# Attention projections as five single-pass products of split operands, and expert weights split in eight pieces, in a tokenizer, attention and mixture-of-experts kernel

## What is computed

```python
h = tok_ref(x, freq_bands, W)          # sin and cos of 2 pi x f for 6 bands, (4, 512, 3*6*2*192) @ W.T -> (4, 512, 192)
h = concatenate([cls_tok, h])          # 513 tokens for each of 4 images
h = h + attn(layernorm(h), Wq, Wk, Wv, Wf, bf, Wo, gamma, beta)
h = h + ffn(layernorm(h), ...)         # 8 routed experts, top 2, and a shared expert of 768, mixed by alpha

def attn(x, ...):                      # linear attention with a forget gate, M = 64
    q = (elu(x @ Wq) + 1) / 8;  k = elu(x @ Wk) + 1;  v = x @ Wv
    c = clip(cumsum(log(sigmoid(x @ Wf + bf))), -20, 20)
    M = exp(c) * cumsum(exp(-c) * k v);  z = exp(c) * cumsum(exp(-c) * k)
    h = (q M) / (q z + 1e-6)
    return (norm(h) * gamma + beta) @ Wo
```

## Time and profile before

| | |
|---|---|
| median of 3 runs | 570.83 us (570.6 to 571.26) |
| the profiled execution | 570.71 us |
| its span | 568.9 us |
| PE busy | 555.4 us, 98% |
| DVE busy | 363.0 us, 64% |
| ACT busy | 245.9 us, 43% |
| POOL busy | 174.0 us, 31% |
| L1312, feature projection | 292.0 us in 1,728 records |
| granted PE clock, mean | 0.994 of full speed |

### The profile page before, as it was taken

The page is one execution under the profiler, slowest core; times in us unless marked ns, Lnnn a source line. Parts: engine busy times, 40 slices in busy tenths (PEclk is TensorE's granted clock), DMA queues, the critical chain, the costliest instruction groups (busy, mean ns, idle before and its releaser), DMA issues.

```text
span 568.9 us, 9027 instructions
## 1 busy us (share of the span) xinstructions
PE 555.4 (98%) x3247; PEld 510.8 (90%) x3247; DVE 363.0 (64%) x1040; ACT 245.9 (43%) x343; POOL 174.0 (31%) x200
## 2 busy tenths in 40 slices
PE   5999999999999999999999999999999999999997
PEld 5998999799999989999979899977888889999965
DVE  7736787532968736779761787376787546666537
ACT  3465364654225753442575523254224134545410
POOL 6413133122225311674311461001300504454410
PEclk9998999999999999999999999999998999999999
DMA  8900067000000000210000010330100561531164
GB/s 330 323 21 20 3 216 243 20 10 20 20 18 20 20 0 11 75 56 1 1 0 10 20 37 20 98 126 23 62 2 1 185 206 54 164 95 52 55 199 152
DMA packets 23487, 42.48 MB, mean 75 GB/s; under 512 B 2502, under 2 KB 15044, under 8 KB 23348
## 3 DMA queue, kind: packets, MB, share of 16 engines
q1 hardware_dynamic: 19560, 33.31, 18.1%
q0 software_dynamic: 3472, 8.07, 4.0%
q10 hardware_dynamic: 412, 0.53, 0.4%
HBM read 31.74 MB, written 14.79 MB: 82 GB/s over the span
## 4 chain that ended last, share of the span: by engine, by line
PE 90%; DVE 5%; ACT 3%; DMA 1%; issue 1%; POOL 0%; ACTq 0%; DVEq 0%
PE ps L1312 47%; PE ps L1505 4%; PE ps L1391 2%; PE ps L1557 2%; PE ps L1559 2%; PE ps L1467 2%; PE ps L1469 2%; PE ps L1470 2%; PE ps L1468 2%; PE ps L1471 2%; PE ps L1368 2%; PE ps L1535 1%; PE ps L1537 1%; PE ps L1536 1%; PE ps L1539 1%; PE ps L1538 1%
## 5 line engine op out<-in xcount | busy, mean ns | idle before, releaser
L1312 PE MATMUL ps<-w_tok,feat 128*128 128x192 f32 x1728 | 292.0, 330 | 7.5 <-ACT feat L469 6.3
L1312 PEld LDWEIGHTS ps<-w_tok,feat 128*128 128x128 f32 x1728 | 284.0, 192 | 11.0 <-issue 10.6
L403 POOL TENSOR_SCALAR feat<-fx 128x512 int32<-128x512 f32 x108 | 93.2, 878 | 204.7 <-PE ps L1312 201.3
L478 ACT ACTIVATE feat<-feat 128x1536 f32<-128x1536 f32 x35 | 51.9, 1484 | 118.6 <-DVE feat L773 116.0
L769 DVE SCALAR_TENSOR_TENSOR feat<-fx,feat 128x512 f32<-128x512 f32 x105 | 76.6, 782 | 1.9 <-POOL feat L403 1.5
L481 ACT ACTIVATE feat<-feat,half_pi 128x1536 f32<-128x1536 f32 x35 | 54.6, 1561 | 0.0
L439 POOL DMA_INDIRECT ydram<-yr,xs x39 | 37.4, 959 | 54.9 <-DVE yr L1085 54.9
L433 POOL DMA_INDIRECT slots<-pay_a,posi x17 | 18.4, 1082 | 74.2 <-DVE posi L1012 70.8
L773 DVE TENSOR_SCALAR feat<-feat 128x1536 int32<-128x1536 int32 x35 | 37.5, 1070 | 1.2
L1505 PE MATMUL ps<-w_down,hid_ring 128*128 128x192 f32 x192 | 36.4, 334 | 0.8 <-issue 0.4
L585 ACT ACTIVATE s_ring<-ps 128x512 f32<-128x512 f32 x24 | 14.4, 599 | 52.1 <-PE ps L1471 52.1
(11 more groups left out here) (277 smaller groups left out, 857.2 us busy)
## 6 DMA issues: line engine op xcount, KB each, us to landing
slots<-in_blank SPq DMA_DIRECT2D x1, 5031.0 KB, 18.7
...
```

Source lines behind the costliest of these rows:

```text
L403: ins = pool.tensor_scalar(feat[:, k % SLOTS, i, :].bitcast(I32), x[:, x_block(k), :], f_col[:, fi:fi + 1], 1.0, ALU.mult, ALU.mult)
L478: act.activation(feat[:, k % SLOTS, 0:3, :], feat[:, k % SLOTS, 0:3, :], ACT.Sin, scale=TWO_PI).then_inc(sin_ready, 1)
L1312: ins = pe.matmul(ps[:, TOK[a % 2][t // 2], (t % 2) * D:(t % 2 + 1) * D], feat[:, k % SLOTS, i, t * P:(t + 1) * P], w_tok[:, k, i, :], sta ...
```

## The change

The attention weights (q and k, forget twice, V, Wo: 640 columns) leave the packed constants and come as one transfer of their own, the last 64 rows twice. ACT and DVE split them once, `split_attention`, in the CLS batch between sines(0,2) or remainders(0,2) and attn1(0). The token side is split as well: in attn1 ACT writes the two high parts and DVE subtracts them, in attn6 DVE scales one half and ACT the other, ACT writes the high parts and DVE subtracts. The buffers are those of X01 and X23 (`operands(a)`). Both layernorms before these steps write the last 64 columns twice. The head outputs go to a part of r (`heads`) and no longer to xn. The forget, q/k, V and Wo products are five f32r products each, with 128 stationary rows: `by_columns` over 512 tokens, `by_rows` over 192 output columns for one tile of 128 tokens. The experts' weights are split in eight pieces of half the size, ACT's at chunks 4, 4, 4, 7, 7, 9, 10, 10 and DVE's one chunk later; their transfers stay four pairs.

```diff
 NYR = 4
-EP = 4
+EL = 4
+EP = 8
 SP_ = 2
...
 Q_LN2, Q_LN3 = Q_X2 - 1, Q_X3 - 1
-Q_HI = (4, 7, 10, 13)
-Q_LO = (5, 8, 11, 14)
+Q_HI = (4, 4, 4, 7, 7, 9, 10, 10)
+Q_LO = (5, 5, 5, 8, 8, 10, 11, 11)
+A_QK, A_F, A_V, A_O = slice(0, 2 * M), slice(2 * M, 4 * M), slice(4 * M, 4 * M + D), slice(4 * M + D, 4 * M + 2 * D)
+AW = 4 * M + 2 * D
...
         H = sb("H", [P, B, NT, D])
-        xn = sb("xn", [P, NT, D])
+        xn = sb("xn", [P, NT, XD])
         pay_a = [sb(f"pay_a{i}", [P, NT + 1, ROW]) for i in range(2)]
         pay_b = sb("pay_b", [P, NT + 1, ROW])
-        xt_a = sb("xt_a", [P, T])
+        raw_w = pay_b[:, :, :].rearrange("p t c -> p (t c)")[:, 0:2 * AW].rearrange("p (h n) -> p h n", h=2)
         v = sb("v", [P, NT, D + 1])
...
         at = r[:, 0:4, :]
-        xt_b = r[DB:P, R_K, :]
+        heads = r[:, 0:2, :].rearrange("p k t -> p (k t)")[:, 0:NT * D].rearrange("p (i d) -> p i d", d=D)
...
                 W, TP, nt = width(a)
+                xh_a_, _, xh_b_, _ = operands(a)
                 act.wait_ge(xpose1, a + 1)
-                act.activation(xt_a[:, 0:W], ps[:, A0, 0:W], ACT.Copy).then_inc(xta_ready, 1)
+                if a >= 1:
+                    act.wait_ge(split_done, SP_)
+                act.activation(xh_a_, ps[:, A0, 0:W], ACT.Copy).then_inc(xah_ready, 1)
+                act.activation(xh_b_, ps[:, A1, 0:W], ACT.Copy).then_inc(xah_ready, 1)
+            def split_attention():
+                act.wait_ge(watt_in, 16)
+                act.activation(aw_hi[:, :], raw_w[:, 0, :], ACT.Copy)
+                act.activation(aw_b[:, :], raw_w[:, 1, :], ACT.Copy).then_inc(att_hi, 1)
...
                 W, TP, nt = width(a)
+                xh_a_, _, xh_b_, _ = operands(a)
                 act.wait_ge(xpose2, a + 1)
-                act.activation(xt_a[:, 0:W], ps[:, A0, 0:W], ACT.Identity, bias=gb_a[:, 1:2],
-                               scale=gb_a[:, 0:1]).then_inc(nta_ready, 1)
+                for dst in (r[:, R_E, 0:W], xh_a_):
+                    ins = act.activation(dst, ps[:, A0, 0:W], ACT.Identity, bias=gb_a[:, 1:2], scale=gb_a[:, 0:1])
+                ins.then_inc(na_ready, 1)
+                act.wait_ge(tb_ready, a + 1)
+                act.activation(xh_b_, r[:, R_PHI, 0:W], ACT.Copy).then_inc(nb_ready, 1)
...
             def expert_hi(p):
-                act.wait_ge(eraw_in, 32 * EP)
+                act.wait_ge(eraw_in, 32 * EL)
                 cut = slice(p * NE // EP, (p + 1) * NE // EP)
...
                     take_ranks(B)
-                if q in Q_HI:
-                    expert_hi(Q_HI.index(q))
+                for p in range(EP):
+                    if Q_HI[p] == q:
+                        expert_hi(p)
...
         def _(dve):
-            def layernorm(src, dst, a, which, TP, nt, done, twice=False, parts=(0, 1, 2)):
+            def layernorm(src, dst, a, which, TP, nt, done, parts=(0, 1, 2)):
...
                     for i in range(nt):
+                        dve.tensor_scalar(dst[0:TP, i, D:XD], src[0:TP, i, P:D], mv[0:TP, i, 0:1],
+                                          y[0:TP, i:i + 1], ALU.subtract, ALU.mult)
                         ins = dve.tensor_scalar(dst[0:TP, i, 0:D], src[0:TP, i, 0:D], mv[0:TP, i, 0:1],
                                                 y[0:TP, i:i + 1], ALU.subtract, ALU.mult)
-                        if twice:
-                            ins = dve.tensor_scalar(dst[0:TP, i, D:XD], src[0:TP, i, P:D], mv[0:TP, i, 0:1],
-                                                    y[0:TP, i:i + 1], ALU.subtract, ALU.mult)
                     ins.then_inc(done, 1)
...
                 W, TP, nt = width(a)
-                dve.wait_ge(xpose1, a + 1)
-                dve.tensor_copy(xt_b[:, 0:W], ps[0:DB, A1, 0:W]).then_inc(xtb_ready, 1)
+                xh_a_, xl_a_, xh_b_, xl_b_ = operands(a)
+                dve.wait_ge(xah_ready, 2 * a + 1)
+                dve.tensor_tensor(xl_a_, ps[:, A0, 0:W], xh_a_.bitcast(F32), ALU.subtract)
+                dve.wait_ge(xah_ready, 2 * a + 2)
+                dve.tensor_tensor(xl_b_, ps[:, A1, 0:W], xh_b_.bitcast(F32), ALU.subtract).then_inc(xal_ready, 1)
+            def split_attention():
+                dve.wait_ge(att_hi, 1)
+                dve.tensor_tensor(aw_lo[:, :], raw_w[:, 0, :], aw_hi[:, :].bitcast(F32), ALU.subtract)
+                dve.tensor_tensor(aw_b[DB:P, :], raw_w[DB:P, 1, :], aw_b[DB:P, :].bitcast(F32),
+                                  ALU.subtract).then_inc(att_split, 1)
...
                     c0 = (i % 2) * (D + 1)
-                    ins = dve.tensor_scalar(xn_[0:TP, i, 0:D], ps[0:TP, AV_BANK[i // 2], c0:c0 + D],
+                    ins = dve.tensor_scalar(heads[0:TP, i, :], ps[0:TP, AV_BANK[i // 2], c0:c0 + D],
                                             rden[0:TP, i:i + 1], None, ALU.mult)
                 ins.then_inc(hh_ready, 1)
                 dve.wait_ge(hh_ready, a + 1)
             def norm_heads(a, parts=(0, 1, 2)):
                 W, TP, nt = width(a)
-                layernorm(normed(a), normed(a), a, 1, TP, nt, hn_ready, parts=parts)
+                layernorm(heads, normed(a), a, 1, TP, nt, hn_ready, parts=parts)
...
                 W, TP, nt = width(a)
+                xh_a_, xl_a_, xh_b_, xl_b_ = operands(a)
                 dve.wait_ge(xpose2, a + 1)
-                dve.tensor_scalar(xt_b[:, 0:W], ps[0:DB, A2, 0:W], gb_b[:, 0:1], gb_b[:, 1:2], ALU.mult,
-                                  ALU.add).then_inc(ntb_ready, 1)
+                dve.tensor_scalar(r[:, R_PHI, 0:W], ps[:, A2, 0:W], gb_b[:, 0:1], gb_b[:, 1:2], ALU.mult,
+                                  ALU.add).then_inc(tb_ready, 1)
+                dve.wait_ge(na_ready, a + 1)
+                dve.tensor_tensor(xl_a_, r[:, R_E, 0:W], xh_a_.bitcast(F32), ALU.subtract)
+                dve.wait_ge(nb_ready, a + 1)
+                dve.tensor_tensor(xl_b_, r[:, R_PHI, 0:W], xh_b_.bitcast(F32), ALU.subtract).then_inc(nl_ready, 1)
...
                     places(B, [2])
-                if q in Q_LO:
-                    expert_lo(Q_LO.index(q))
+                for p in range(EP):
+                    if Q_LO[p] == q:
+                        expert_lo(p)
             dve.memset(hidt[:, :, D:2 * P], 0.0).then_inc(hidt_zero, 1)
...
                 for i in range(nt):
-                    ins = pe.transpose(ps[0:DB, A1, i * P:i * P + TP], xn_[0:TP, i, P:D], ident[0:TP, 0:TP])
+                    ins = pe.transpose(ps[:, A1, i * P:i * P + TP], xn_[0:TP, i, P:XD], ident[0:TP, 0:TP])
                 ins.then_inc(xpose1, 1)
+            def by_columns(o, a, cols):
+                xh_a_, xl_a_, xh_b_, xl_b_ = operands(a)
+                pe.matmul(o, aw_hi[:, cols], xh_a_, start=True, stop=False)
+                pe.matmul(o, aw_lo[:, cols], xh_a_, start=False, stop=False)
+                pe.matmul(o, aw_hi[:, cols], xl_a_, start=False, stop=False)
+                pe.matmul(o, aw_b[:, cols], xh_b_, start=False, stop=False)
+                return pe.matmul(o, aw_b[:, cols], xl_b_, start=False, stop=True)
+            def by_rows(o, a, cols, i, first):
+                TP = width(a)[1]
+                xh_a_, xl_a_, xh_b_, xl_b_ = (t[:, i * P:i * P + TP] for t in operands(a))
+                pe.matmul(o, xh_a_, aw_hi[:, cols], start=first, stop=False, skip_group_check=True)
+                pe.matmul(o, xh_a_, aw_lo[:, cols], start=False, stop=False, skip_group_check=True)
+                pe.matmul(o, xl_a_, aw_hi[:, cols], start=False, stop=False, skip_group_check=True)
+                pe.matmul(o, xh_b_, aw_b[:, cols], start=False, stop=False, skip_group_check=True)
+                return pe.matmul(o, xl_b_, aw_b[:, cols], start=False, stop=True, skip_group_check=True)
             def values(a, first):
                 W, TP, nt = width(a)
-                tiles_ = range(first, min(first + 2, nt))
-                def place(i):
-                    return ps[0:TP, (A1, A0)[i // 2], (i % 2) * D:(i % 2 + 1) * D]
-                for i in tiles_:
-                    pe.matmul(place(i), xt_a[:, i * P:i * P + TP], wv_a[:, :], start=(i % 2 == 0), stop=False,
-                              skip_group_check=True)
-                for i in tiles_:
-                    ins = pe.matmul(place(i), xt_b[:, i * P:i * P + TP], wv_b[:, :], start=False, stop=True,
-                                    skip_group_check=True)
+                for i in range(first, min(first + 2, nt)):
+                    o = ps[0:TP, (A1, A0)[i // 2], (i % 2) * D:(i % 2 + 1) * D]
+                    ins = by_rows(o, a, A_V, i, i % 2 == 0)
                 ins.then_inc((v01_psum, v23_psum)[first // 2], 1)
             def attn2(a):
                 W, TP, nt = width(a)
-                pe.wait_ge(xta_ready, a + 1)
-                pe.wait_ge(xtb_ready, a + 1)
-                pe.matmul(ps[:, A0, 0:W], wff_a, xt_a[:, 0:W], start=True, stop=False)
```

(24 more changed lines are left out.)

42 lines of the change are left out of this document (20 added, 22 removed).

## The result

The changed kernel takes **596.9 us** (median of 4 runs, 596.1 to 598.4) against 571.0 of the kernel before in the same comparison: 1.0448 times the time, 95% interval 1.0424 to 1.0472. It is 25.9 us slower, where 5.4 were forecast and 582.0 was the end of the range. The sign and most of the places of the waits were right; the size was not. The profiled execution has a span of 595.9 us, 27.0 more than before.

The account below looks back on a forecast made before the run. TensorE was taken to bound the kernel, never stopping, so savings return only while its feeders have slack. The terms +0.1 +2.0 +2.0 +1.4 +0 = +5.5 on 570.7 gave 576.2 us, range 566 to 582.

Parts of the forecast that it names:

- What bounds the kernel, and what is taken from TensorE: TensorE never stops; its shorter attention products save 3.45 us per batch, 13.8 in four, plus 0.4 in the CLS batch.
- First place, attn1 to attn3: VectorE's subtractions wait for ScalarE's copies behind the sines; TensorE then waits about 2.7 us at attn3, ending 0.1 behind.
- Second place: attn5 to attn8: late VectorE work delays the residual and layernorm, +2.0 us each for batches 2 and 3, +0.1 for batch 1.
- the term for places[2] and the layernorm: VectorE work before attn8, batches 2 and 3: places[2] 2.2 us, residual and layernorm 7.1, ready near 264.7.
- Third place: Last batch's attention between chunk products: TensorE waits 3.3 us for the late silu; +1.4 us in all.
- The sum: Added time over token batches, chunk part and remainder: +5.5 on 570.7, giving 576.2 us.
- The rival on the clock: New TensorE waits lower the clock: one further fall 577.9 us, two 579 to 580; chance 0.15 for two or more.
- the prediction's own sign of being wrong: Over the whole kernel: the forecast is wrong if, among other signs, the clock falls at more than two new places.
- The rival's own sum: The time given for one further clock fall after TensorE's new waits: 577.9 us.
- Narrow products are slow: V and Wo: 192-column products take 0.325 us each, about +6 us per batch, 594 us; chance 0.10.
- The rest: CLS batch's weight split taken as 0 (-0.4 to +1.5 us); experts' eight pieces worth 0 (-0.2 to +0.7).

Follow-up runs that it names:

- act_early: The changed kernel with ScalarE's attn1 moved ahead of sines(b,2) and its attn6 ahead of sines(b,7): 570.2 us, 0.9958 times the kernel before.
- early_attn1: The changed kernel with only ScalarE's attn1 moved ahead of sines(b,2): 1.0173 times the kernel before.
- early_attn6: The changed kernel with only ScalarE's attn6 moved ahead of sines(b,7): 1.0340 times the kernel before.
- experts_alone: The kernel before with only the expert weights' split in eight pieces, nothing of the attention part: 0.9992 times the kernel before.

## Why the prediction was wrong, point by point

- **What bounds the kernel, and what is taken from TensorE**: right. By-rows products at 0.11, scores reached early. The Trainium skill ("TensorE: Matmul & The Clock Gate", section "LDWEIGHTS (loading the stationary operand)") has a load take the number of its columns divided by 1.2 in ns, by which 128 columns are an estimated 107 ns. The 0.11 us agree with that. The isolated gap of the Trainium skill (same page, section "Back-to-back issue gap"), N/2.4 + 2.5 ns for N columns, gives an estimated 83 ns for 192. These products take 111 ns in a stream.
- **First place, attn1 to attn3**: mechanism right, shown by act_early and early_attn1; VectorE idled 3.50 us before its first subtraction, where 4 were forecast. 2.7 us of wait in each batch were forecast, 3.67, 0.62 and 2.64 measured. Batch 2 is short where the clock fell at its router (192 to 200 us), so that TensorE came late; in early_attn6, which has no fall there, it waits 3.4.
- **Second place**: mechanism right, one term mis-sized. The heads' layernorm 0.3 us and Wo up to 0.4 (measured 0.31, 0.41 and 0.31; 0.2). Attn8: 2.0 us forecast for batches 2 and 3, 4.56 and 1.62 measured. In batch 2 the term for places[2] and the layernorm took the durations of the earlier trace rows for work that had moved beside GpSimd's rounding, where it took 2.9 us longer.
- **Third place**: 3.3 us forecast, 3.08 measured; the heads' layernorm 0.7 forecast, 0.86 measured. The last batch's wait of 1.65 us at attn8 was not in the sum.
- **The sum left the clock out**, and this is the step that failed. The sum has no term for the clock. The rival on the clock had the right mechanism, but was priced at one or two falls of 1.6 us each, from the one fall of the earlier trace rows. The runs show both too small. Besides the one at 44 us there are seven stretches at the lower level against one before, among them four behind waits; the prediction's own sign of being wrong, a fall at more than two new places, came true. And three of the four last some 10 us, with the scores and the projection in them, and cost TensorE up to 5 us each; the short ones last 3.4 us and cost the 1.6 or so of the one in the earlier trace rows. The waits themselves were 20.8 us, where the parts of the sum hold some 18 (8.1 at attn3, 4 at attn8, 3.3 at the silu, 1.6 at the heads' layernorm, 1.2 at Wo): nearly right. The clock then took 20.8 more, by the sum above, against a forecast of none.
- **The rival's own sum**: one fall on 576.2 is 577.8, not 577.9; nothing hangs on it.
- **Rival "Narrow products are slow"** gave 594, the nearest number, for a reason that the trace refutes. The products start 0.11 us apart. That it came near is chance.
- **The rest**: experts nothing, held (experts_alone). CLS nothing: no wait of TensorE appeared there, and no run tests it by itself.
